# Statistics of two normalisations put behind copies and row maxima, and registers loaded ahead of waits

## What is computed

```
def _L1_ffn_ref(x, ...):                 # block 3
    h_expert = swiglu(flat @ expert_in_w.T)
    for e in range(8):                   # two experts a token
        routed += comb[:, e:e+1] * (h_expert @ expert_out_weight[e].T)
    return out_shared + routed

def _expert(x, ...):                     # block 5: 8 experts, two a token
    q, k, v = split(x @ Wqkv.T + bqkv)   # 8 heads of 32
    attn = softmax(q * scale @ k.T)      # over all 1354 tokens
    ctx = (attn @ v) @ Wo.T + bo
    x = layernorm(x + ctx) * g1 + be1
    h = gelu(x @ W1.T + bf1)
    h = gelu(h @ W2.T + bf2)
    return layernorm(x + h) * g2 + be2

def _moe_forward(x, ...):                # block 7: 8 experts, two a token
    h = relu(x @ W1[e] + b1[e])
    y = h @ W2[e] + b2[e]
    y = (y - mean(y)) / sqrt(var(y) + 1e-5) * gamma[e] + beta[e]
    return sum over the two experts of gate * y
```

## Time and profile before

| | us |
|---|---|
| median of 3 runs | 3034.55 |
| lowest, highest | 3026.40, 3037.34 |
| profiled execution, its own time | 3007.01 |
| its span, first to last instruction | 3005.0 |
| PE busy in the span | 2405.0 (80%) |
| DVE busy | 1550.8 (52%) |
| ACT busy | 1152.6 (38%) |
| POOL busy | 500.1 (17%) |
| transformer loop, about | 1588 to 2671 |
| routed experts' loop, about | 1216 to 1291 |
| last experts' loop, about | 2887 to 2979 |

### The profile page before, as it was taken

The page is one execution under the profiler, slowest core; times in us unless marked ns, Lnnn a source line. Parts: engine busy times, 40 slices in busy tenths (PEclk is TensorE's granted clock), DMA queues, the critical chain, the costliest instruction groups (busy, mean ns, idle before and its releaser), DMA issues. The chain is left out here.

```text
span 3005.0 us, 52688 instructions
## 1 busy us (share of the span) xinstructions
PE 2405.0 (80%) x18555; PEld 2004.3 (67%) x18555; DVE 1550.8 (52%) x3102; ACT 1152.6 (38%) x2239; POOL 500.1 (17%) x812
## 2 busy tenths in 40 slices
PE   6989599769977849974877999999999999963356
PEld 4868489769956734764865777777777777753344
DVE  3646522232236751144435777777777777742355
ACT  3333222112213321132214666666666666624433
POOL 0000022122202100600001122222222222210043
PEclk9999799779988969976998999999999999976678
DMA  5000023134341121411764231334244452012144
GB/s 137 1 1 1 24 88 94 54 99 150 93 104 56 47 92 48 129 53 42 277 255 130 80 101 37 101 99 137 60 138 136 115 146 68 26 47 53 57 130 137
DMA packets 136392, 273.54 MB, mean 91 GB/s; under 512 B 33667, under 2 KB 70569, under 8 KB 133061
## 3 DMA queue, kind: packets, MB, share of 16 engines
q1 hardware_dynamic: 117332, 217.49, 23.2%
q0 software_dynamic: 18800, 52.69, 6.7%
HBM read 466.52 MB, written 65.74 MB: 177 GB/s over the span
## 5 line engine op out<-in xcount | busy, mean ns | idle before, releaser
L2244 PE MATMUL tx_ring<-g_ident,tx_p 128*128 128x128 f32 x2552 | 401.3, 284 | 51.1 <-DVE tx_p_t L2489 20.8
L2244 PEld LDWEIGHTS tx_ring<-g_ident,tx_p 128*128 128x128 f32 x2552 | 286.8, 142 | 162.8 <-DVE tx_p_t L2489 57.7
L2482 DVE TENSOR_REDUCE tx_neg_max<-tx_scores 128x1 f32<-128x1354 f32 x232 | 361.5, 1559 | 16.2 <-PE tx_scores L2232 16.2
L2378 ACT ACTIVATE tx_p<-tx_scores,tx_neg_max 128x1354 f32<-128x1354 f32 x232 | 322.4, 1390 | 87.9 <-DVE tx_neg_max L2482 85.2
L2489 DVE COPY tx_p_t<-tx_ring 128x512 f32<-128x512 f32 x464 | 301.5, 680 | 46.6 <-PE tx_ring L2244 46.6
L2385 ACT ACTIVATE tx_p_t<-tx_ring 128x384 f32<-128x384 f32 x232 | 113.1, 488 | 269.9 <-PE tx_ring L2244 266.2
L2232 PE MATMUL tx_scores<-tx_keys,tx_queries 96*128 96x512 f32 (+1 forms) x696 | 202.7, 400 | 15.7 <-DMA tx_queries<-tx_q_hi 11.2
L2284 PE MATMUL tx_ring<-tx_p_t,tx_values 128*32 128x128 f32 x5104 | 152.0, 274 | 18.7 <-ACT tx_p_t L2385 17.9
L2284 PEld LDWEIGHTS tx_ring<-tx_p_t,tx_values 128*32 128x32 f32 x5104 | 135.9, 110 | 29.8 <-ACT tx_p_t L2385 29.0
L2232 PEld LDWEIGHTS tx_scores<-tx_keys,tx_queries 96*128 96x128 f32 x696 | 115.7, 193 | 26.6 <-issue 16.1
L192 PE MATMUL ln_turned<-g_ident,g_xn 128*128 128x128 f32 x176 | 39.2, 407 | 117.6 <-DVE g_xn L179 117.6
(11 more groups left out here) (961 smaller groups left out, 5189.9 us busy)
## 6 DMA issues: line engine op xcount, KB each, us to landing
tx_keys<-expert_keys SPq DMA_DIRECT2D x696, 169.5 KB
lv1e_w<-in_L_ffn_W SPq DMA_DIRECT2D x232, 256.0 KB
tx_w<-in_L_ffn_W SPq DMA_DIRECT2D x58, 1024.0 KB
lv0e_w<-in_L_ffn_W SPq DMA_DIRECT2D x200, 256.0 KB
tx_values<-expert_values SPq DMA_DIRECT2D x58, 704.0 KB
tx_rows<-in_L_ffn_rows SPq DMA_DIRECT2D x29, 640.0 KB, 3.9
g_adj_t<-in_adj_t POOLq DMA_DIRECT2D x3, 3872.0 KB, 22.1
expert_values<-kv_v SPq DMA_DIRECT2D x8, 1408.0 KB, 5.7
```

The costliest lines, as they stand in the source:

```text
L2244: last = nc.tensor.transpose(ring[u % 2][:, (t - t0) * P:(t - t0 + 1) * P], p[n % 2][:, t * P:(t + 1) * P], g.ident[:])
L2378: nc.scalar.activation(p[n % 2][:, 0:N], sc[n % 2][:, 0:N], ACT.Exp, bias=neg_max[:, n % 4:n % 4 + 1], accum_out=row_sum[:, i % 2, hd:hd + ...
L2482: nc.vector.tensor_reduce(neg_max[:, n % 4:n % 4 + 1], sc[n % 2][:, 0:N], AX_X, ALU.max, negate=True)\
```

## The change

In the transformer loop, on DVE alone: `middle_stats` moves from slot 1 (behind `scale_bias`) to slot 2, between the two copies and the row maximum; `end_stats` moves from slot 5 to slot 6, behind the row maximum; in slot 6 `inverse(i, 1)` moves between `end_stats` and `end_norm`, ahead of `add_second`. The condition on the row maximum stands outside `if i < tiles` now, which changes nothing. In the two experts' loops the register load of a tile's owner is called earlier: on PE ahead of the next transposes, on ACT ahead of `deviation(i)` (for tile i+3), on DVE ahead of the wait in `result`.

```diff
--- before.py
+++ after.py
@@ -1235,6 +1235,7 @@
                 last.then_inc(shared_full, 1)
             turn(0)
             for i in range(tiles):
+                of(i)
                 if i + 1 < tiles:
                     turn(i + 1)
                 project(i)
@@ -2568,15 +2569,14 @@
                     if i < tiles:
                         keep_turned(i, hd, 0)
                         keep_turned(i, hd, 1)
-                        if HEADS * i + hd + AHEAD < heads:
-                            row_max(HEADS * i + hd + AHEAD)
+                    if hd == 2 and 0 < i <= tiles:
+                        middle_stats(i - 1)
+                    if HEADS * i + hd + AHEAD < heads:
+                        row_max(HEADS * i + hd + AHEAD)
                     if hd == 0 and 0 < i <= tiles:
                         context(i - 1, 1)
-                    if hd == 1:
-                        if i + 1 < tiles:
-                            scale_bias(i + 1)
-                        if 0 < i <= tiles:
-                            middle_stats(i - 1)
+                    if hd == 1 and i + 1 < tiles:
+                        scale_bias(i + 1)
                     if hd == 2:
                         if 0 < i <= tiles:
                             middle_norm(i - 1)
@@ -2584,15 +2584,15 @@
                         inverse(i, 0)
                     if hd == 4 and i < tiles:
                         context(i, 0)
-                    if hd == 5 and i >= 2:
-                        end_stats(i - 2)
                     if hd == 6:
+                        if i >= 2:
+                            end_stats(i - 2)
+                        if i < tiles:
+                            inverse(i, 1)
                         if i >= 2:
                             end_norm(i - 2)
                         if 0 < i <= tiles:
                             add_second(i - 1)
-                        if i < tiles:
-                            inverse(i, 1)
             back.mix(dve, spare + ring)
 
         @block.gpsimd
@@ -2868,6 +2868,7 @@
 
             bring(0)
             bring(1)
+            of(2)
             keep_rows(0)
             keep_rows(1)
             hide(0)
@@ -2877,6 +2878,8 @@
                     bring(i + 2)
                 if i + 1 < tiles:
                     hide(i + 1)
+                if i + 3 < tiles:
+                    of(i + 3)
                 deviation(i)
 
         @block.vector
```

## The result

| | before | after |
|---|---|---|
| median of 5 runs, us | 3033.73 | 3011.10 |
| lowest, highest | 3026.40, 3037.34 | 3008.34, 3015.10 |
| ratio over all runs, 95% interval | | 0.9930 [0.9920, 0.9941] |
| profiled execution, its own time | 3007.01 | 3008.34 |
| its span | 3005.0 | 3006.4 |

The change takes 22.6 us off by the medians (0.9925), and 0.9930 of 3033.7 is 21.2 us; the ratio is taken over all runs and not from the medians. The two profiled executions do not show the gain: the one of before, 3007.01, is none of the five runs of its column and lies 19 us under the lowest of them, the one of after is one of its five. So they are read stage by stage. The transformer stage is 14.6 us shorter, the last loop of this one execution is 10.4 us longer. The first is the change, the second is looked at further down.

The account below looks back on a forecast made before the run. PE was taken to bound the transformer loop, a chain of waits the last experts' loop. Gains 4.5 + 7.3 + 8.3 + 1.0 = 21.1 us, from 3034.55 to 3013.5 us; range 3000 to 3028.

Parts of the forecast that it names:

- Part 1: Transformer loop, first normalisation's statistics moved from slot 1 to slot 2: 0.16 us a tile, 4.5 us over 28 tiles.
- slot 3's lateness of 0.32: Slot 3's second copy on DVE, due at 2115.48, came at 2115.80; this 0.32 us lateness was to disappear.
- the 0.16 reaches PE's path: After slot 3's row maximum: its 0.16 us gain passes by exponent and ACT's copy to the product with the values.
- Part 2: Transformer loop, second normalisation's statistics moved to slot 6 and inverse ahead of the addition: 0.27 us a tile, 7.3 us.
- The port rule: Slot 6: DVE and POOL share an exclusive port lock, so POOL's power step waits for the inverse's copy, up to 0.23 us.
- The first rival: The hole before slot 6's addition is too small, addition 0.25 us or more late: 14 us less, 3020.5; chance 20%.
- Part 3: Both experts' loops, register loads called ahead of waits: 8.3 us in the last loop, 1 us in the routed loop.
- POOL becomes the bound: Last experts' loop: POOL's alternating sends and fetches, 2.57 us a tile, limit it; 6.2 us won over 21 tiles.
- In the last 7 tiles, without a fetch, 7 x 0.35 = 2.4: Last experts' loop, final seven tiles where POOL fetches nothing: 0.35 us a tile won, 2.4 us in all.
- The term for the first 21 tiles, 6.2: Last experts' loop, tiles with fetches: 60.2 us falls to 21 x 2.57, a gain of 6.2 us.
- the 0.61 of the earlier trace: Last experts' loop: DVE's 0.61 us idle before the addition, taken as the load's cost; 0.35 off, 0.25 stays.
- Rival 2: Last loop held by something else, as sends' landing or weight loads: register loads give 0 to 3 us, 3021; chance 10%.

Follow-up runs that it names:

- e1: Kernel before with only `middle_stats` moved, from slot 1 to slot 2: ratio 0.9985 to before, tile 36.29 us against 36.56.
- e2: Kernel before with only `end_stats` and `inverse(i, 1)` moved: ratio 0.9977 to before, tile 36.29 us against 36.56.
- e7: Both normalisations' moves without the register loads, plus one extra 128x1 POOL instruction before the second deviation: ratio 0.9973 to before, tile 36.22 us.
- e5: Both statistics moved as in the change, `inverse(i, 1)` left behind the addition, no loads moved: ratio 0.9989 to before, tile 36.25 us.
- e6: First statistics moved, `end_stats` left in slot 5, `inverse(i, 1)` put ahead of the addition, no loads moved: ratio 0.9950 to before, tile 35.95 us.
- e9: Kernel before with only the last experts' loop's register loads moved (ACT and DVE): ratio 0.9978 to before, first to last send 73.7 us against 77.7.
- e3: Kernel before with only the register loads moved, in both experts' loops: ratio 0.9973 to before, tile 36.57 us.
- e10: Whole change, with POOL fetching twelve tiles ahead of the last loop instead of eight: ratio 0.9933 to before, first to last send 74.8 us.
- e12: Whole change with `end_stats` back in slot 5, twelve tiles fetched ahead and four result places in the last loop: ratio 0.9920 to before.
- e11: Whole change, with four places for results in the last loop instead of two: ratio 0.9921 to before, first to last send 71.0 us.

## Why the prediction was right, and where not

**Total.** 21.1 us were forecast and 22.6 measured; 3013.5 against 3011.1. None of the rivals' times came in. That the total is so close is partly luck: part 1 and the routed loop gave more than forecast, the last loop less, and these errors nearly cancel.

**Part 1** was forecast at 0.16 us a tile and gave 0.27 (e1). The two steps of the working came out: the row maximum of slot 2 is 0.16 late, and slot 3's lateness of 0.32 is gone, so the next row maximum is 0.19 early. The size that was off is the step from there, "the 0.16 reaches PE's path": the product with the values came 0.26 early, 0.07 more than the row maximum. Two chains lead to it, and the prediction followed only the one by the row maximum and the exponent. The other goes by PE and ACT: in slot 4 PE's second transposes need the ring's bank that ACT drains of the normalised rows turned in slot 3, and this drain (L2426, L2427 in after) comes earlier:

```profile
2117.14 0.80 ACT L2426 ACTIVATE tx_x_t<-tx_ring,tx_cols 128x128 f32<-128x128 f32 x2
```

```profile
2116.41 0.81 ACT L2427 ACTIVATE tx_x_t<-tx_ring,tx_cols 128x128 f32<-128x128 f32 x2
```

From the slot-7 row maximum it starts at 16.23 in after and 16.53 in before, 0.30 earlier (0.30 in e1 too), PE's second transposes start 0.05 behind its end in both kernels, and the scores, the third unit, ACT's copy of it and the product follow. DVE's own copies of slot 4 came only 0.20 earlier.

**Part 2** was forecast at 0.27 and gave 0.27 (e2). The margin was read rightly: the addition is 0.03 late by the working and 0.08 in the trace (0.18 early, where part 1 had brought 0.26), and e7 shows that there is nothing left. The row maximum of slot 7 is 0.30 early within its slots, 0.29 forecast. What the prediction did not see is that the move of the statistics was not needed. It wrote "The win is behind it: the inverse", and yet costed both moves as one. e5 and e6 tell them apart.

**The port rule.** In the kernel after, the inverse's copy starts at 2133.11, beside POOL's first small step: 0.30 us for that step, where it takes 0.22 in e5 with DVE quiet, and 0.25 for the copy, 0.23 alone. Beside POOL's longer operations the copy takes 0.43 to 0.77, and in the tiles shown it ends just behind POOL's: 0.10 behind the residual in before, 0.08 behind y in e6, where POOL started first (2126.45) and the copy, begun at 2126.49, ended at 2127.26. The Trainium skill, SBUF — State Buffer, section "SBUF: two separate sides", has one of the two engines wait while the other holds the port pair for a whole instruction. With these long operations the traces agree. With the small step of the kernel after they do not show it: 0.22 and 0.23 one behind the other would be 0.45 us, and both are done 0.30 us after the first began. The first rival had priced the rule at up to 0.23 a tile: POOL's power step started behind the copy, at 2133.48, and POOL lost no more than those 0.08.

**Part 3** was forecast at 8.3 us for the last loop and gave 5.9 (e9), at 1.0 for the routed loop and gave some 2 (e3 less e9, across two chips, so no more than a hint; from first to last send the routed loop takes 66.8 to 67.6 us in e3 and e10 to e12 and 68.5 to 69.0 in before and the kernels that leave its load alone). The sends of the last loop did come 2.57 us apart, as written, but not for the reason written. The step that failed is "POOL becomes the bound". Its sum counts 0.33 us in which POOL, by its own row, waits for DVE; POOL's turn in the routed loop is also 2.57, so it could not have gone faster, but DVE's turn of 2.17 and 0.41 us is as long, with a fetch and without. So "In the last 7 tiles, without a fetch, 7 x 0.35 = 2.4" measured 0.7 in e9 (17.5 to 16.8 us from the send of tile 21 to the last). The term for the first 21 tiles, 6.2, measured 3.3 in e9 (60.2 to 56.9) and 6.0 in e11 (54.2), where no landing holds a result: what it left out is the landings. And the 0.61 of the earlier trace rows was not the price of a load. One tile earlier in the same trace, where PE was in time, the addition has the 0.41 of e9 with the load still behind the wait:

```profile
2935.17 0.43 DVE L2892 TENSOR_TENSOR nee_y<-nee_row,new_rows 128x256 f32<-128x256 f32 x1 [0.41 <-issue]
```

So 0.41 is what is left in both orders, and what is gone is the rest, the tiles in which the product was late. Whether ACT's load or DVE's did that was not tried one by one; the loads of the kernel after answer to the earlier trace rows:

```profile
L1567 ACTq TENSOR_LOAD <-ne_owner x29: 272/278/480, 2875.2 to 2967.4; - x29
L1567 DVEq TENSOR_LOAD <-ne_owner x29: 300/304/547, 2875.2 to 2975.2; - x29
```

ACT's median is 278 ns, where it was 450; DVE's is as before.

**Rival 2** said that the last loop is held by something else, as the sends' landing. Something else it was, DVE, at the very pace that was given for POOL, so that the gain came all the same. The landing of the sends does not hold every tile, but it costs 3.0 us in e9 and 4.5 in e10.

## What to carry to other kernels

When an edit moves several things into a hole, cost each move by itself: here one of them, the small copy taken out from between two critical instructions, was the whole gain, and the other only used up the margin. A register load moved ahead of a wait helps only as long as the engine still waits there. Look where the load itself runs before its price is taken from the idle time: here it lay under the instruction before in both orders, and the gap was the steps behind it. Two engines with the same time for a tile are told apart by the idle time before each, and better by taking work from one of them: e10 took the fetches from POOL, and the pace stayed.

## What had not been expected

- The same kernel before has a median of 3033.7 us in one set of runs and of 3004.0 to 3006.4 in three others, 0.9% apart, more than the change is worth. Its profile, 3007.01, fits the other three. The tile of 36.56 against 36.02 us, which 21 and 20 of the 28 tiles of the two traces repeat within 0.02, was the measure that could be compared across them.
- The same operation, the 128x128 copy of the inverse, took 0.23, 0.25, 0.43, 0.49 and 0.77 us, by what POOL was doing beside it.
- Landing of the sends in the last loop lay between 2.4 and 6.0 us (e11) for the same 128 rows.
